# Pairwise feature products on one core: engine programs written as loops, and features copied by GpSimd ahead of the transposes

## Chip, cores and metric

The kernel runs on one core of one Trainium2 chip. The metric is the device time of one execution in microseconds; three runs of the kernel before gave 505.67, 505.77 and 505.79 us, a median of 505.77.

## What is computed

The input `r_x` holds 512 samples of 40 features with 128 numbers each, and `L0_rec_W` is a 128x128 matrix, all in fp32. Each feature is multiplied by the matrix, and then each of the 780 pairs of different features is multiplied element by element. The output has 512 x 780 x 128 numbers, 204.47 MB.

```python
proj = jnp.einsum('bnd,ed->bne', x, W)
out = proj[:, PAIR_I, :] * proj[:, PAIR_J, :]   # all i < j of 40
```

## The kernel before

The 512 samples are four **tiles** of 128, one sample to a partition. A tile's 40 features are 20 **groups** of two, and are worked from the last feature to the first. All x stays in one SBUF tensor, `feats`; the projected features are written over x in place.

The stages run on different engines and are tied by counting semaphores.

- **SP** issues the loads first: tile 0 in three pieces (features 36 to 39, 28 to 35, 0 to 27, L99), then tiles 1 to 3 (L101). After that it issues one store for each **chunk** of 65 pairs, 12 to a tile and 48 in all, once VectorE has it ready (L106 to L108). All these transfers are in SP's queue, in this order.
- **TensorE** transposes the two features of a group into PSUM (`turn`, L122, reading `feats`), and multiplies the transposed features of the group before by the turned matrix (`project`, L128). The two steps alternate, with two buffers for each. For tile 0 it waits for the pieces, and for the rest once for all of tiles 1 to 3 (L157).
- **ACT** (ScalarE) copies each transposed group out of PSUM to `x_turned` (L174), and each projected group back into `feats` (L180).
- **VectorE** (DVE) multiplies. A chunk is made of 2 to 11 `tensor_tensor` instructions (L197), each for one feature i and a run of features j, with both inputs in `feats`; 49 to a tile. The chunk goes to one of three output buffers, `products`, and needs the store of three chunks before to have landed (L207, L212). Within a chunk it waits on `proj_ready` where an instruction needs a group not yet seen (L196). Tile 0 is written out; tiles 1 to 3 are a loop on the chip (L209).
- **GpSimd** (POOL) makes the identity matrix for the transposes (L115, L117) and then does nothing.

TensorE's and ACT's programs for all 80 groups are written out, one instruction after another.

## Time and profile before

| | before |
|---|---|
| median of 3 runs | 505.77 us |
| the profiled execution, its own time | 505.62 us |
| its span in the profile | 503.8 us |
| VectorE busy | 433.6 us (86%), 196 instructions |
| TensorE, ACT busy | 63.4 us, 54.2 us |
| GpSimd busy | 0.7 us, 6 instructions |
| moved by DMA | 215.11 MB, mean 427 GB/s |

The span runs from the first to the last event of the profiled execution; 1.8 us of its own time lie outside of it. Busy shares are averages over the whole span: TensorE and ACT do all their work in the first 80 us. The time of TensorE's matmuls is modelled, and the span of a GpSimd instruction is rough.

### The profile page before, as it was taken

What the parts mean: (1) busy time and instruction counts of PE and PEld (TensorE: products, weight loads), DVE (VectorE), ACT (ScalarE), POOL (GpSimd) and SP (SyncE); (2) the same over time, 40 slices, a digit from 0 to 9 for tenths busy, and PEclk for the clock granted to TensorE, in tenths of its full rate; (3) what the DMA queues carried; (4) which work ended last, traced back from release to release, by engine and by line L of the source; (5) the groups of instructions that cost most, each with busy time, mean ns of one, the idle gap of its engine ahead of it and who ended that gap; (6) DMA issues with size and microseconds to landing.
All of it is one profiled execution on the core that took longest, in us unless ns stands there. A gap on an engine that the chain in (4) does not pass through costs nothing.

```text
span 503.8 us, 1684 instructions
## 1 busy us (share of the span) xinstructions
PE 63.4 (13%) x481; PEld 57.6 (11%) x481; DVE 433.6 (86%) x196; ACT 54.2 (11%) x162; POOL 0.7 (0%) x6
## 2 busy tenths in 40 slices
PE   6659993000000000000000000000000000000000
PEld 5648982000000000000000000000000000000000
DVE  3987899899899989998898999899899989998930
ACT  5638982000000000000000000000000000000000
POOL 0000000000000000000000000000000000000000
PEclk9969997555555555555555555555555555555555
DMA  8999999999999999999999999999999999999997
GB/s 356 424 403 441 427 424 429 447 428 425 434 444 428 428 433 444 428 428 431 447 428 428 431 447 428 428 431 441 433 428 428 436 439 431 428 428 439 433 433 312
DMA packets 7926, 215.11 MB, mean 427 GB/s; under 512 B 880, under 2 KB 1008, under 8 KB 1264
## 3 DMA queue, kind: packets, MB, share of 16 engines
q1 hardware_dynamic: 7776, 214.96, 99.3%
q8 instruction: 4, 0.07, 0.0%
q10 hardware_dynamic: 144, 0.07, 0.0%
q14 instruction: 2, 0.02, 0.0%
HBM read 10.55 MB, written 204.47 MB: 427 GB/s over the span
## 4 chain that ended last, share of the span: by engine, by line
DMA 62%; DVE 25%; issue 5%; DVEq 2%; PE 1%; ACT 0%
DMA out_dram<-products 62%; DVE products L197 25%; DVEq L57 2%; DMA w_in<-in_L_rec_W_dram 1%; PE proj_ps L134 0%; PE turned_ps L125 0%; DVEq L197 0%; DVEq L196 0%; DVEq L209 0%; PE w_ps L143 0%; ACT feats L180 0%; DVEq L212 0%
## 5 line engine op out<-in xcount | busy, mean ns | idle before, releaser
L197 DVE TENSOR_TENSOR products<-feats 128x1280 f32 (+36 forms) x196 | 433.6, 2275 | 49.2 <-DMA out_dram<-products 41.1
L134 PE MATMUL proj_ps<-w_turned,x_turned 128*128 128x128 f32 x320 | 54.7, 295 | 0.6 <-ACT x_turned L174 0.5
L134 PEld LDWEIGHTS proj_ps<-w_turned,x_turned 128*128 128x128 f32 x320 | 43.3, 197 | 5.3 <-ACT x_turned L174 2.1
L125 PE MATMUL turned_ps<-identity,feats 128*128 128x128 f32 x160 | 31.7, 285 | 11.3 <-DMA feats<-in_r_x_dram 10.3
L174 ACT COPY x_turned<-turned_ps 128x256 f32<-128x256 f32 x80 | 30.0, 377 | 12.3 <-PE turned_ps L125 12.1
L180 ACT COPY feats<-proj_ps 128x256 f32<-128x256 f32 x80 | 29.8, 373 | 10.0 <-PE proj_ps L134 4.7
L125 PEld LDWEIGHTS turned_ps<-identity,feats 128*128 128x128 f32 x160 | 20.9, 148 | 12.3 <-issue 10.5
L170 ACT ACT_TABLE_LOAD x1 | 1.3, 1283 | 1.2 <-PEq L224 1.2
L143 PE MATMUL w_ps<-identity,w_in 128*128 128x128 f32 x1 | 0.4, 447 | 4.2 <-DMA w_in<-in_L_rec_W_dram 4.2
L143 PEld LDWEIGHTS w_ps<-identity,w_in 128*128 128x128 f32 x1 | 0.2, 182 | 4.2 <-issue 4.2
L170 ACT COPY w_turned<-w_ps 128x128 f32<-128x128 f32 x1 | 0.3, 266 | 2.3 <-PE w_ps L143 2.3
L117 POOL TENSOR_SCALAR_AFFINE_SELECT identity<-identity 128x128 f32<-128x128 f32 x1 | 0.3, 294 | 0.2 <-POOL identity L115 0.2
L115 POOL MEMSET identity<- 128x128 f32 x1 | 0.2, 204 | 0.3 <-POOLq L224 0.3
L224 POOL MEMSET const-bfloat16-1.0<- 128x1 bf16 x1 | 0.1, 102 | 0.0
L224 POOL MEMSET const-uint8-127<- 128x1 uint8 x1 | 0.1, 102 | 0.0
L224 POOL MEMSET const-float32-1.0<- 128x1 f32 x1 | 0.1, 99 | 0.0
L224 POOL MEMSET const-float32-0.0<- 128x1 f32 x1 | 0.1, 98 | 0.2 <-issue 0.2
## 6 DMA issues: line engine op xcount, KB each, us to landing
out_dram<-products SPq DMA_DIRECT2D x48, 4160.0 KB, 20.5
feats<-in_r_x_dram SPq DMA_DIRECT2D x3, 2560.0 KB, 19.5
feats<-in_r_x_dram SPq DMA_DIRECT2D x1, 1792.0 KB, 8.3
feats<-in_r_x_dram SPq DMA_DIRECT2D x1, 512.0 KB, 4.3
feats<-in_r_x_dram SPq DMA_DIRECT2D x1, 256.0 KB, 3.2
w_in<-in_L_rec_W_dram ACTq DMA_DIRECT2D x1, 64.0 KB, 3.3
```

What stands on the lines that cost most here:

```text
L57: with ExitStack() as ctx:
L115: pool.memset(identity[:, :], 0.0).then_inc(identity_zeroed, 1)
L117: pool.affine_select(out=identity[:, :], in_=identity[:, :], compare_op=ALU.not_equal, fill=1.0, base=0, pattern=[[-1, P]], channel_multip ...
L125: last = pe.transpose(turned_ps[group % 2][:, n - a, :], feats[:, tile, n, :], identity[:, :])
L134: last = pe.matmul(proj_ps[group % 2][:, k, :], x_turned[group % 2][:, k, :], w_turned[:, :], start=True, stop=True)
L143: pe.transpose(w_ps[:, :], w_in[:, :], identity[:, :]).then_inc(w_in_ps, 1)
L170: act.copy(w_turned[:, :], w_ps[:, :]).then_inc(w_ready, 1)
L174: act.copy(x_turned[group % 2][:, :, :], turned_ps[group % 2][:, 0:GROUP, :]).then_inc(x_turned_ready, 1)
L180: act.copy(feats[:, tile, a:b, :], proj_ps[group % 2][:, 0:GROUP, :]).then_inc(proj_ready, 1)
L197: last = dve.tensor_tensor(products[k % SLOTS][:, place:place + count, :], feats[:, tile, i:i + 1, :].broadcast_to([P, count, DIM]), feats ...
L224: nc = _bacc.Bacc("TRN2", target_bir_lowering=False, num_devices=1)
```

## The change

TensorE's and ACT's 80 groups become loops on the chip of two groups a turn, with what does not fit the loop ahead of it and behind it. An instruction of such a loop names the same place on every turn, so GpSimd first copies each group's two features from `feats` to one of two fixed buffers, `staged`, and TensorE's transposes read that. GpSimd waits for the transposes of two groups before (`group_turned`, which starts at 2), and for the loads: the pieces of the first tile worked on, and then once for the three other tiles. VectorE's four tiles are one loop; it waits for projected groups once at a chunk's start, for all that the chunk needs, where it waited between the instructions of a chunk. The first waits that had no count behind them are met by counts given in advance (`proj_ready` starts at 2), and TensorE's wait for `proj_ready` is there for every group. The tiles are worked from the last to the first, so `feats` is walked in falling order. The loads of the first tile now count on the semaphores of the three output buffers.

```diff
-        feats = sbuf("feats", [P, tiles, FEATURES, DIM])
+        feats = sbuf("feats", [P, features, DIM])
         products = [sbuf(f"products{s}", [P, CHUNK, DIM]) for s in range(SLOTS)]
+
+        staged = [sbuf(f"staged{k}", [P, GROUP, DIM]) for k in range(2)]
...
-            for k, (a, b) in enumerate(FIRST_LOADS):
-                sp.dma_start(feats[:, 0, a:b, :], x[0:P, a:b, :]).then_inc(first_loaded[k], 16)
-            for tile in range(1, tiles):
-                sp.dma_start(feats[:, tile, :, :], x[tile * P:(tile + 1) * P, :, :]).then_inc(tiles_loaded, 16)
-
-            for tile in range(tiles):
+            last = (tiles - 1) * P
+            for s, (a, b) in enumerate(PIECES):
+                at = (tiles - 1) * FEATURES
+                sp.dma_start(feats[:, at + a:at + b, :], x[last:last + P, a:b, :]).then_inc(slot_free[s], 16)
+            for tile in reversed(range(tiles - 1)):
+                sp.dma_start(feats[:, tile * FEATURES:(tile + 1) * FEATURES, :],
+                             x[tile * P:(tile + 1) * P, :, :]).then_inc(tiles_loaded, 16)
+
+            for turn in range(tiles):
+                tile = tiles - 1 - turn
                 for k in range(CHUNKS):
                     low, high = chunk_range(k)
-                    sp.wait_ge(chunk_ready, tile * CHUNKS + k + 1)
+                    sp.wait_ge(chunk_ready, turn * CHUNKS + k + 1)
                     sp.dma_start(out[tile * P:(tile + 1) * P, low:high, :],
-                                 products[k % SLOTS][:, :, :]).then_inc(stored[k % SLOTS], 16)
+                                 products[k % SLOTS][:, :, :]).then_inc(slot_free[k % SLOTS], 16)
 
             for slot in range(SLOTS):
-                sp.wait_ge(stored[slot], 16 * tiles * ROUNDS)
+                sp.wait_ge(slot_free[slot], 16 + 16 * tiles * ROUNDS)
...
+            def stage_two(pair):
+
+                for k in range(2):
+                    pool.wait_ge(group_turned, pair * 2 + (k + 1))
+                    pool.tensor_copy(staged[k][:, :, :],
+                                     feats[:, bass.ds(pair * -(2 * GROUP) + (features - (k + 1) * GROUP), GROUP), :]
+                                     ).then_inc(group_staged, 1)
+
+            pairs = [(FEATURES - a) // (2 * GROUP) for a, b in PIECES]
+            pool.wait_ge(slot_free[0], 16)
+            with pool.Fori(0, pairs[0]) as pair:
+                stage_two(pair)
...
+            pool.wait_ge(tiles_loaded, 16 * (tiles - 1))
+            with pool.Fori(pairs[2], groups // 2) as pair:
+                stage_two(pair)
...
-            def turn(tile, group):
-                a, b = group_range(group)
-                for n in range(a, b):
-                    last = pe.transpose(turned_ps[group % 2][:, n - a, :], feats[:, tile, n, :], identity[:, :])
+            def turn(group, k):
+
+                pe.wait_ge(group_staged, group + 1)
+                for n in range(GROUP):
+                    last = pe.transpose(turned_ps[k][:, n, :], staged[k][:, n, :], identity[:, :])
                 last.then_inc(group_turned, 1)
 
-            def project(before, group):
-                pe.wait_ge(x_turned_ready, before + (group + 1))
-                if group >= 2:
-
-                    pe.wait_ge(proj_ready, before + (group - 1))
-                for k in range(GROUP):
-                    last = pe.matmul(proj_ps[group % 2][:, k, :], x_turned[group % 2][:, k, :], w_turned[:, :],
+            def project(group, k):
+                pe.wait_ge(x_turned_ready, group + 1)
+                pe.wait_ge(proj_ready, group + 1)
+                for n in range(GROUP):
+                    last = pe.matmul(proj_ps[k][:, n, :], x_turned[k][:, n, :], w_turned[:, :],
                                      start=True, stop=True)
                 last.then_inc(group_projected, 1)
 
-            def last_banks_left(before):
-                pe.wait_ge(proj_ready, before + GROUPS)
-
+            pe.sem_inc(group_turned, 2)
             pe.wait_ge(identity_made, 1)
             pe.wait_ge(w_loaded, 16)
             pe.transpose(w_ps[:, :], w_in[:, :], identity[:, :]).then_inc(w_in_ps, 1)
-
-            starts = {group_of(b - 1): k for k, (a, b) in enumerate(FIRST_LOADS)}
-            pe.wait_ge(first_loaded[0], 16)
             turn(0, 0)
             pe.wait_ge(w_ready, 1)
-            for group in range(1, GROUPS):
-                if group in starts:
-                    pe.wait_ge(first_loaded[starts[group]], 16)
-                turn(0, group)
-                project(0, group - 1)
-            project(0, GROUPS - 1)
-            last_banks_left(0)
-
-            pe.wait_ge(tiles_loaded, 16 * (tiles - 1))
-            for tile in range(1, tiles):
-                turn(tile, 0)
-                for group in range(1, GROUPS):
-                    turn(tile, group)
-                    project(tile * GROUPS, group - 1)
-                project(tile * GROUPS, GROUPS - 1)
-                last_banks_left(tile * GROUPS)
+            with pe.Fori(0, groups // 2 - 1) as pair:
+                turn(pair * 2 + 1, 1)
+                project(pair * 2, 0)
+                turn(pair * 2 + 2, 0)
+                project(pair * 2 + 1, 1)
+            turn(groups - 1, 1)
+            project(groups - 2, 0)
+            project(groups - 1, 1)
...
+            act.sem_inc(proj_ready, 2)
...
-            def carry_turned(tile, group):
-                act.wait_ge(group_turned, tile * GROUPS + group + 1)
-                act.copy(x_turned[group % 2][:, :, :], turned_ps[group % 2][:, 0:GROUP, :]).then_inc(x_turned_ready, 1)
-
-            def carry_projected(tile, group):
-
-                a, b = group_range(group)
-                act.wait_ge(group_projected, tile * GROUPS + group + 1)
-                act.copy(feats[:, tile, a:b, :], proj_ps[group % 2][:, 0:GROUP, :]).then_inc(proj_ready, 1)
-
-            for tile in range(tiles):
-                carry_turned(tile, 0)
-                for group in range(1, GROUPS):
-                    carry_turned(tile, group)
-                    carry_projected(tile, group - 1)
-                carry_projected(tile, GROUPS - 1)
+            def carry_turned(group, k):
+                act.wait_ge(group_turned, group + 3)
+                act.copy(x_turned[k][:, :, :], turned_ps[k][:, 0:GROUP, :]).then_inc(x_turned_ready, 1)
+
+            def carry_projected(group, k):
+
+                act.wait_ge(group_projected, group + 1)
+                act.copy(feats[:, bass.ds(group * -GROUP + (features - GROUP), GROUP), :],
+                         proj_ps[k][:, 0:GROUP, :]).then_inc(proj_ready, 1)
+
+            carry_turned(0, 0)
+            with act.Fori(0, groups // 2 - 1) as pair:
+                carry_turned(pair * 2 + 1, 1)
+                carry_projected(pair * 2, 0)
+                carry_turned(pair * 2 + 2, 0)
+                carry_projected(pair * 2 + 1, 1)
+            carry_turned(groups - 1, 1)
+            carry_projected(groups - 2, 0)
+            carry_projected(groups - 1, 1)
...
-            def multiply_chunk(tile, k, seen):
-
-                for i, j, count, place in chunk_rows(*chunk_range(k)):
-                    if group_of(i) >= seen:
-                        seen = group_of(i) + 1
-                        dve.wait_ge(proj_ready, tile * GROUPS + seen)
-                    last = dve.tensor_tensor(
-                        products[k % SLOTS][:, place:place + count, :],
-                        feats[:, tile, i:i + 1, :].broadcast_to([P, count, DIM]),
-                        feats[:, tile, j:j + count, :], ALU.mult)
-                last.then_inc(chunk_ready, 1)
-                return seen
-
-            seen = 0
-            for k in range(CHUNKS):
-                if k >= SLOTS:
-                    dve.wait_ge(stored[k % SLOTS], 16 * (k // SLOTS))
-                seen = multiply_chunk(0, k, seen)
-            with dve.Fori(1, tiles) as tile:
-                seen = 0
+            with dve.Fori(0, tiles) as turn:
+                at = turn * -FEATURES + (tiles - 1) * FEATURES
                 for k in range(CHUNKS):
-                    dve.wait_ge(stored[k % SLOTS], 16 * ROUNDS * tile + 16 * (k // SLOTS))
-                    seen = multiply_chunk(tile, k, seen)
+                    dve.wait_ge(slot_free[k % SLOTS], turn * (16 * ROUNDS) + 16 * (k // SLOTS + 1))
+                    if k == 0 or groups_for(k) > groups_for(k - 1):
+                        dve.wait_ge(proj_ready, turn * GROUPS + (2 + groups_for(k)))
+                    for i, j, count, place in chunk_rows(k):
+                        last = dve.tensor_tensor(
+                            products[k % SLOTS][:, place:place + count, :],
+                            feats[:, bass.ds(at + i, 1), :].broadcast_to([P, count, DIM]),
+                            feats[:, bass.ds(at + j, count), :], ALU.mult)
+                    last.then_inc(chunk_ready, 1)
```

VectorE's instructions, their sizes and their order within a tile, the sizes of the loads and the 48 stores are the same.

On TensorE, the start of its program before; the names are the PSUM buffers written and the operands read:

```order
L143 MATMUL w_ps<-identity,w_in 128x128 [waits w_loaded,identity_made]
L125 MATMUL turned_ps0<-identity,feats 128x128 [waits first_loaded0]
L125 MATMUL turned_ps0<-identity,feats 128x128
L125 MATMUL turned_ps1<-identity,feats 128x128 [waits w_ready]
L125 MATMUL turned_ps1<-identity,feats 128x128
L134 MATMUL proj_ps0<-w_turned,x_turned0 128x128 [waits x_turned_ready]
L134 MATMUL proj_ps0<-w_turned,x_turned0 128x128
L125 MATMUL turned_ps0<-identity,feats 128x128 [waits first_loaded1]
L125 MATMUL turned_ps0<-identity,feats 128x128
```

The loop of the change on TensorE, whole:

```order
L159 MATMUL turned_ps1<-identity,staged1 128x128 [waits group_staged]
L159 MATMUL turned_ps1<-identity,staged1 128x128
L163 REGISTER_ALU
L166 MATMUL proj_ps0<-w_turned,x_turned0 128x128 [waits proj_ready,x_turned_ready]
L166 MATMUL proj_ps0<-w_turned,x_turned0 128x128
L157 REGISTER_ALU
L159 MATMUL turned_ps0<-identity,staged0 128x128 [waits group_staged]
L159 MATMUL turned_ps0<-identity,staged0 128x128
L166 MATMUL proj_ps1<-w_turned,x_turned1 128x128 [waits proj_ready,x_turned_ready]
L166 MATMUL proj_ps1<-w_turned,x_turned1 128x128
L176 REGISTER_ALU
L176 COMPARE_AND_BRANCH
```

The transposes read `staged` and wait for it; their order against the projections is as before.

On GpSimd, which had nothing after the identity matrix, the loop of the change for the groups of the three later tiles (30 turns; the loops for the first tile's pieces are alike):

```order
L150 UNCONDITIONAL_BRANCH [waits tiles_loaded]
L150 ISA
L135 ISA [waits group_turned]
L135 COPY staged0<-feats 128x256
L134 REGISTER_ALU
L135 ISA [waits group_turned]
L135 COPY staged1<-feats 128x256
L150 REGISTER_ALU
L150 COMPARE_AND_BRANCH
```

The wait for the loads has moved here from TensorE, and each group adds one copy of 128 x 256 numbers.

On VectorE, the first chunk of the first tile before:

```order
L197 TENSOR_TENSOR products0<-feats 128x128 [waits proj_ready]
L197 TENSOR_TENSOR products0<-feats 128x256 [waits proj_ready]
L197 TENSOR_TENSOR products0<-feats 128x384
L197 TENSOR_TENSOR products0<-feats 128x512 [waits proj_ready]
L197 TENSOR_TENSOR products0<-feats 128x640
L197 TENSOR_TENSOR products0<-feats 128x768 [waits proj_ready]
```

And in the change:

```order
L214 ISA
L219 ISA [waits slot_free0]
L221 ISA [waits proj_ready]
L221 ISA
L221 TENSOR_TENSOR products0<-feats 128x128
L221 ISA
L221 TENSOR_TENSOR products0<-feats 128x256
L221 ISA
L221 TENSOR_TENSOR products0<-feats 128x384
```

One wait for six groups stands ahead of the chunk in place of six waits within it, and an address is set before each multiply.

## Rows read from the trace of the kernel before

**Rows 1.** The page: span, and its slices of DMA share and rate.

```profile
span 503.8 us, 1684 instructions
...
DMA  8999999999999999999999999999999999999997
GB/s 356 424 403 441 427 424 429 447 428 425 434 444 428 428 433 444 428 428 431 447 428 428 431 447 428 428 431 441 433 428 428 436 439 431 428 428 439 433 433 312
```

**Rows 2.** DMA queues: packets, MB, share of 16 engines.

```profile
q1 hardware_dynamic: 7776, 214.96, 99.3%
q8 instruction: 4, 0.07, 0.0%
...
q14 instruction: 2, 0.02, 0.0%
```

**Rows 3.** Stretches: length, busy time (instructions) by engine, TensorE clock, DMA share, GB/s.

```profile
0.00:2.00 2.00, 0.00 (x0) 0.00 (x0) 0.00 (x0) 0.84 (x1) 0.70 (x6) 1.00 0.13 17
2.00:4.00 2.00, 0.00 (x0) 0.00 (x0) 0.00 (x0) 0.44 (x1) 0.00 (x0) 1.00 0.91 288
25.00:26.00 1.00, 0.00 (x0) 0.00 (x0) 1.00 (x2) 0.00 (x0) 0.00 (x0) 0.50 1.34 369
26.00:27.00 1.00, 0.00 (x0) 0.00 (x0) 1.00 (x2) 0.00 (x0) 0.00 (x0) 0.50 0.92 246
27.00:28.00 1.00, 0.00 (x0) 0.00 (x0) 1.00 (x2) 0.00 (x0) 0.00 (x0) 0.50 0.91 335
28.00:29.00 1.00, 0.00 (x0) 0.00 (x0) 1.00 (x1) 0.00 (x0) 0.00 (x0) 0.50 0.75 320
40.00:480.00 440.00, 38.02 (x304) 34.50 (x302) 403.12 (x174) 33.27 (x102) 0.00 (x0) 0.55 1.00 433
```

**Rows 4.** Timeline of VectorE: start, length, what, count, idle before and its releaser.

```profile
7.21 0.29 DVE L197 TENSOR_TENSOR products<-feats 128x128 f32<-128x128 f32 x1 [7.21 <-ACT feats L180]
8.28 27.40 DVE L197 TENSOR_TENSOR products<-feats 128x256 f32<-128x256 f32 x21 [0.77 <-ACT feats L180]
41.04 9.03 DVE L197 TENSOR_TENSOR products<-feats 128x1920 f32<-128x1920 f32 x4 [5.36 <-DMA out_dram<-products]
50.86 8.96 DVE L197 TENSOR_TENSOR products<-feats 128x2048 f32<-128x2048 f32 x3 [0.79 <-DMA out_dram<-products]
...
90.20 8.96 DVE L197 TENSOR_TENSOR products<-feats 128x1024 f32<-128x1024 f32 x3 [0.86 <-DMA out_dram<-products]
```

**Rows 5.** Waits: who waited for whom, us in total, times, longest.

```profile
DVE products L197 <- DMA out_dram<-products: 41.1, 42, 5.4
```

**Rows 6.** The page's issues: KB each, median us from issue to landing.

```profile
out_dram<-products SPq DMA_DIRECT2D x48, 4160.0 KB, 20.5
```

**Rows 7.** The page's groups of VectorE and GpSimd: busy, mean ns of one, idle before.

```profile
L197 DVE TENSOR_TENSOR products<-feats 128x1280 f32 (+36 forms) x196 | 433.6, 2275 | 49.2 <-DMA out_dram<-products 41.1
...
L117 POOL TENSOR_SCALAR_AFFINE_SELECT identity<-identity 128x128 f32<-128x128 f32 x1 | 0.3, 294 | 0.2 <-POOL identity L115 0.2
L115 POOL MEMSET identity<- 128x128 f32 x1 | 0.2, 204 | 0.3 <-POOLq L224 0.3
L224 POOL MEMSET const-bfloat16-1.0<- 128x1 bf16 x1 | 0.1, 102 | 0.0
```

**Rows 8.** Timeline of ACT, TensorE and SP, same columns as rows 4.

```profile
10.87 0.37 ACT L180 COPY feats<-proj_ps 128x256 f32<-128x256 f32 x1
...
11.60 0.37 ACT L180 COPY feats<-proj_ps 128x256 f32<-128x256 f32 x1
...
12.32 0.37 ACT L180 COPY feats<-proj_ps 128x256 f32<-128x256 f32 x1
...
17.61 18.42 SPq L107 DMA_DIRECT2D out_dram<-products  x3
...
31.31 1.09 PE L125 MATMUL turned_ps<-identity,feats 128*128 128x128 f32 x4 [10.34 <-DMA feats<-in_r_x_dram]
```

More of the change, by code:

```diff
@@ L14 @@
 GROUPS = FEATURES // GROUP
-FIRST_LOADS = [(36, 40), (28, 36), (0, 28)]
+PIECES = [(36, 40), (28, 36), (0, 28)]
 SLOTS = 3
@@ L23, with chunk_rows @@
 ROUNDS = CHUNKS // SLOTS
-assert CHUNKS * CHUNK == PAIRS and ROUNDS * SLOTS == CHUNKS
-assert GROUPS * GROUP == FEATURES and GROUPS % 2 == 0 and GROUP <= BANK_FEATURES
-def group_range(group):
-    return FEATURES - (group + 1) * GROUP, FEATURES - group * GROUP
-def group_of(i):
-    return (FEATURES - 1 - i) // GROUP
+assert CHUNKS * CHUNK == PAIRS and ROUNDS * SLOTS == CHUNKS and len(PIECES) == SLOTS
+assert GROUPS * GROUP == FEATURES and GROUPS % 2 == 0 and 2 * GROUP <= BANK_FEATURES
 def chunk_range(k):
     return PAIRS - (k + 1) * CHUNK, PAIRS - k * CHUNK
-def chunk_rows(low, high):
+def chunk_rows(k):
+    low, high = chunk_range(k)
     rows = []
@@ L48, in chunk_rows, with groups_for @@
     return rows
+def groups_for(k):
+    return (FEATURES - 1 - chunk_rows(k)[-1][0]) // GROUP + 1
 def pairwise_products(nc, x, w, out):
@@ L55, in pairwise_products @@
     assert x.shape[0] == tiles * P and 2 <= tiles <= 4
+    features = tiles * FEATURES
+    groups = tiles * GROUPS
     with ExitStack() as ctx:
@@ L79, in pairwise_products @@
         w_loaded = sem("w_loaded")
-        first_loaded = [sem(f"first_loaded{k}") for k in range(len(FIRST_LOADS))]
+        slot_free = [sem(f"slot_free{s}") for s in range(SLOTS)]
         tiles_loaded = sem("tiles_loaded")
@@ L86, in pairwise_products @@
         w_ready = sem("w_ready")
+        group_staged = sem("group_staged")
         group_turned = sem("group_turned")
@@ L91, in pairwise_products @@
         chunk_ready = sem("chunk_ready")
-        stored = [sem(f"stored{s}") for s in range(SLOTS)]
         block = ctx.enter_context(nc.Block())
@@ new lines, in _ @@
+            pool.wait_ge(slot_free[0], 16)
+            with pool.Fori(0, pairs[0]) as pair:
+                stage_two(pair)
+            pool.wait_ge(slot_free[1], 16)
+            with pool.Fori(pairs[0], pairs[1]) as pair:
+                stage_two(pair)
+            pool.wait_ge(slot_free[2], 16)
+            with pool.Fori(pairs[1], pairs[2]) as pair:
+                stage_two(pair)
+            pool.wait_ge(tiles_loaded, 16 * (tiles - 1))
+            with pool.Fori(pairs[2], groups // 2) as pair:
+                stage_two(pair)
```

## The prediction

> **What bounds the kernel now.** I read the page's slices first. The 16 DMA engines are at 0.9 or more of the time in every slice but the first and the last [rows 1], and SP's queue, which holds all loads and stores, takes 99.3% of what they can give [rows 2]. From 40 to 480 us they move 433 GB/s at a share of 1.00 [rows 3]. So the kernel runs at the pace of its stores, and the question is whether the queue ever runs dry.
>
> VectorE's timeline gives the rhythm. Its chunks begin at 41.04, 50.86, 60.69 and, three chunks on, 90.20 us, each time when a store has landed [rows 4]: one store each (90.20 - 41.04) / 5 = 9.83 us. Store number n (from 0) lands at 41.04 + 9.83n, so the 48th at 503.1, which is the span. VectorE takes 8.96 to 9.03 us for such a chunk and then idles 0.79 to 0.87 us; 41.1 us of its idle time are waits for stores [rows 4, 5]. A store takes 20.5 us from issue to landing [rows 6], two stores' time, so when VectorE ends a chunk the DMA engines still have the rest of one store and a whole one before them. That is the cover: VectorE may fall behind by some 10 us before the engines stop, and it wins back about 0.8 us with each chunk.
>
> TensorE and ACT are far ahead of need: a group each 0.73 us (copies at 10.87 and 11.60), and TensorE idles 10.34 us until tiles 1 to 3 are there at 31.31 [rows 8].
>
> **The parts that cost nothing by themselves.** *Tiles in falling order, loads on other semaphores*: the same loads in the same order of sizes, the same stores in SP's queue, nothing ahead of them: 0. *TensorE and ACT as loops*: register steps and a branch, some tenths of a us for two groups. If a group took 1.5 us in place of 0.73, 80 would take 120 us and VectorE needs them over 400 us; it is hidden, and it stays hidden as long as VectorE finds its groups. *VectorE's addresses*: tiles 1 to 3 had them already, and ran at the pace of the stores. *The waits at a chunk's start*: VectorE began at 7.21 us, after the first group; now it must have six. ACT's copy of the sixth began at 10.87 and took 0.37 us [rows 8], which is 11.24, and with GpSimd's copy ahead of the transposes and a few register steps I put VectorE's start at 11.7. Three chunks before took from 8.28 to 35.68, with a pause of 5.36 us behind them until the first store had landed at 41.04 [rows 4]. From 11.7 they end near 39, inside that pause. The first store was issued at 17.61 [rows 8]; now it would be near 21, while the loads run until 31.3. So this costs nothing alone, but it spends most of that pause. *The wait for the loads*, now GpSimd's, stops the same groups as it did in TensorE.
>
> **The part that can cost: 80 copies on GpSimd.** No row has GpSimd and VectorE at work together, so the price is bounded. Of one copy, 128x256: a MEMSET of one column takes 102 ns and one of 128 columns 204, that is 0.80 ns a column more, and AFFINE_SELECT, which also reads, 294 ns for 128 columns, 1.5 ns a column [rows 7]. So 256 columns take 0.31 to 0.49 us. TensorE waits for the copy, but a group every 0.8 to 1 us is still enough. What matters is VectorE: both engines read `feats` in SBUF. If they don't hinder each other, the copies cost nothing. If they take turns, a multiply waits for the copy that got in between. Then VectorE loses at least the 0.31 us less the 0.10 us that even one column takes, 0.21; at most 0.49 us and the overlap of two multiplies behind each other as well. That overlap: 196 x 2.275 = 445.9 us of instructions are 433.6 us of busy time [rows 7], 12.3 us over the 148 joints inside chunks, 0.08 us each. The ends are 0.21 and 0.57 us; nearest to a copy that reads and writes lies no row, so I take the middle, 0.39.
>
> **The sum, if they take turns (my forecast).** VectorE is busy without a pause once it is behind, and one copy gets in at each of its multiplies. The first 20 groups are done by 31.3 us (only the first six before VectorE starts); the other 60 then go one to a multiply. Chunks 0 and 1 have 17 multiplies, and 17 + 60 = 77 is reached in chunk 16 (49 in the first tile, 29 in the five chunks 12 to 16). So 74 copies stand in VectorE's way before the end of chunk 16. It ends at 11.7 + 17 x 9.05 + 74s = 165.6 + 74s, with 9.05 us a chunk from the busy time, 433.6 / 48 = 9.03, and a little between. To keep the engines fed it must be issued before store 15 lands, at 41.04 + 9.83 x 15 = 188.5, less the 1.5 us that a transfer takes to begin (the first load was issued at 0.74; the engines have a share of 0.13 up to 2 us and 0.91 from 2 to 4 [rows 3]): 187.0. The loss is 74s - 21.4: at s = 0.39 it is 7.5 us, at 0.57 20.8 us, and nothing below s = 0.29. After chunk 16 VectorE wins back 0.8 us a chunk, but time that the DMA engines stood idle does not come back.
>
> The profiled execution took 505.62 us, 0.15 below the median of 505.77. 505.6 + 7.5 = **513.1 us**. This case's own range is 505.6 to 526.4.
>
> [...]
>
> **The rivals.**
>
> *Side by side.* The two engines don't hinder each other. For it: all of TensorE's, ACT's and VectorE's work from 40 to 60 us ran beside each other and a chunk took 8.96 us, as it did from 90 us on when they were done [rows 4]. Against it: that says nothing of GpSimd. Time 505.6 to 505.8.
>
> *VectorE keeps its place.* A copy gets in only when VectorE pauses. There is one pause a chunk, 0.8 us, room for a copy; a tile needs 20 groups and has 12 chunks. So VectorE comes to a chunk whose groups are missing and waits for them at 0.75 to 1 us each. For a tile this needs 15 to 20 us of pauses where 12 x 0.83 = 10 are free: 5 to 10 us lost for each of three tiles, less the cover of 10 us that is there once and less the groups of the first tile that were done early: 0 to 15 us, 505.6 to 520, middle 510.
>
> *Faster: the engines get back what they miss between 25 and 29 us.* In these four microseconds they moved 369, 246, 335 and 320 GB/s where 433 is their pace [rows 3]: 0.46 MB, 1.1 us. If fetching the long programs is what stands in the way (6 packets of instructions, 0.09 MB [rows 2]), short loops take it away: 504.5. It decides as soon as one such packet sits on the engine that ends last. Against it: the packets are 0.09 of 215 MB, 0.2 us at 433 GB/s, and loads and stores change over in just this stretch. [...]
>
> **How the numbers follow.** A measurement of this kernel can tell 0.2%, 1.0 us. Chances: taking turns 0.52, of which a fifth falls below s = 0.30 and can't be told from no change; side by side 0.28; VectorE keeps its place 0.13, two thirds of it slower; faster 0.07. Slower: 0.42 + 0.09 = 0.51. Same: 0.10 + 0.28 + 0.04 = 0.42. Faster: 0.07. The predicted time is that of the likeliest case, 513.1. The range takes in the first rival and the first case's upper bound with a little for the delays between the engines that no row prices: 505.2 to 528.
>
> **What the profile would show.** Taking turns: copies on GpSimd whose spans run from 0.3 up to a multiply's length, VectorE's start-to-start times longer by about 0.4 us while the copies last, TensorE's and ACT's last group near 190 us instead of 80, no pauses of VectorE between 31 and 190 us, DMA shares under 0.9 in some slices there, and from 190 us on the rhythm of before. Side by side: the last group before 100 us, multiplies at their old pace and a pause again before each chunk. VectorE keeping its place: pauses that end with ACT's copy to `feats`, spread to the end of the run. Faster: no dip between 25 and 29 us. The forecast is wrong if a copy takes far from 0.4 us, if VectorE starts well after 12 us (the first store then comes after the loads have ended and each us late is a us lost), or if two copies get in at one multiply.

## The result, and the profile after

| | before | after |
|---|---|---|
| median of 13 runs each, on one chip | 505.71 us | 506.81 us |
| ratio, with its 95% interval | | 1.0025 (1.0018 to 1.0032) |
| the profiled execution, its own time | 505.62 us | 506.74 us |
| its span | 503.8 us | 504.9 us |
| instructions executed | 1684 | 2550 |
| GpSimd busy | 0.7 us | 159.3 us |

The change costs about 1.1 us. The direction is the forecast one; the size was forecast at 7.5 us. The profile shows nearly all that the forecast case describes, and yet not its loss. This is the page of the kernel after: the span, busy times, the slices of VectorE, GpSimd, ACT and DMA share, queues, the two costliest groups of the engines in question, and the stores.

```profile
span 504.9 us, 2550 instructions
PE 100.6 (20%) x481; PEld 84.7 (17%) x481; DVE 446.2 (88%) x196; ACT 59.8 (12%) x162; POOL 159.3 (32%) x86
...
DVE  0999999999999999998899999899999989998930
ACT  4623222222443200000000000000000000000000
POOL 3969999999799900000000000000000000000000
...
DMA  8999999999999999999999999999999999999996
...
q1 hardware_dynamic: 7776, 214.96, 99.1%
...
q14 instruction: 1, 0.01, 0.0%
...
L221 DVE TENSOR_TENSOR products<-feats 128x1280 f32 (+30 forms) x196 | 446.2, 2343 | 37.7 <-DMA out_dram<-products 24.4
L135 POOL COPY staged<-feats 128x256 f32 (+1 forms) x80 | 158.6, 2024 | 16.5 <-DMA feats<-in_r_x_dram 10.4
...
out_dram<-products SPq DMA_DIRECT2D x48, 4160.0 KB, 20.3
```

GpSimd is busy in 14 slices of 12.6 us, up to 177 us, and ACT as long: before, ACT was done at 80. VectorE's multiplies are busy for 12.6 us more in all [rows 7]. But the DMA share is 0.9 or more in all slices but the first and the last, as before [rows 1]: VectorE's delay never let the queue run dry. The time is lost while the DMA engines look full.

Three views show the form of the delay. First GpSimd's copy alone, in a window before VectorE starts, and then beside VectorE (count: min/median/max in ns, where in us, shapes):

```profile
L135 POOL COPY staged<-feats x6: 397/403/404, 4.1 to 8.8; 128x256 f32 x4, 128x256 f32<-128x256 f32 x2
...
L135 POOL COPY staged<-feats x5: 1921/3656/3922, 59.8 to 72.9; 128x256 f32 x5
```

A copy that takes 0.40 us alone spans a whole multiply beside VectorE: it gets in once for each. VectorE's timeline, and ACT's last group (start, length, what, count, idle before):

```profile
13.17 175.61 DVE L221 TENSOR_TENSOR products<-feats 128x128 f32 x81 [13.17 <-ACT feats L199]
...
189.43 8.96 DVE L221 TENSOR_TENSOR products<-feats 128x2048 f32 x3 [0.64 <-DMA out_dram<-products]
199.26 8.96 DVE L221 TENSOR_TENSOR products<-feats 128x1280 f32 x3 [0.87 <-DMA out_dram<-products]
...
179.06 0.37 ACT L199 COPY feats<-proj_ps 128x256 f32<-128x256 f32 x1 [0.48 <-PE proj_ps L166]
```

VectorE works without a pause from 13.17 to 188.8 us, 81 multiplies of chunks 0 to 17, and the pauses before chunks return at 189.43. Third, stretches that hold one chunk of 3 large multiplies (stretch, length, VectorE's busy time and instructions, TensorE's granted clock, DMA share, GB/s; the x5 counts the neighbours that touch the stretch too): beside the copies, and after them.

```profile
63.10:72.57 9.47, 9.47 (x5) 0.50 0.99 425
...
189.43:198.39 8.96, 8.96 (x3) 0.50 1.03 446
```

The 189.43 chunk is undisturbed: 8.96 us. A chunk beside the copies takes 9.55 us from its first multiply to its last's end, and 9.47 from start to start. So a copy costs VectorE (9.55 - 8.96) / 3 = **0.197 us** a multiply. That is half of what the prediction took for it.

Single stores, first stores 9 and 15 of the kernel before, then stores 0, 9 and 15 of the kernel after and the issue of its store 16 (issue in ns, and where; then time to landing):

```profile
L107 SPq DMA_DIRECT2D out_dram<-products x1: 333/333/333, 109.0 to 109.0; - x1
DMA to landing us min/median/max: 20.5/20.5/20.5
...
L107 SPq DMA_DIRECT2D out_dram<-products x1: 332/332/332, 168.1 to 168.1; - x1
DMA to landing us min/median/max: 20.4/20.4/20.4
```

```profile
L118 SPq DMA_DIRECT2D out_dram<-products x1: 348/348/348, 24.3 to 24.3; - x1
DMA to landing us min/median/max: 15.5/15.5/15.5
...
L118 SPq DMA_DIRECT2D out_dram<-products x1: 332/332/332, 110.6 to 110.6; - x1
DMA to landing us min/median/max: 17.8/17.8/17.8
...
L118 SPq DMA_DIRECT2D out_dram<-products x1: 333/333/333, 170.5 to 170.5; - x1
DMA to landing us min/median/max: 18.8/18.8/18.8
...
L118 SPq DMA_DIRECT2D out_dram<-products x1: 332/332/332, 179.9 to 179.9; - x1
```

Here is where the time goes. Store 0 lands at 39.8 us (before: 41.0) and store 9 at 128.4 (129.5): the kernel after is 1.1 us *ahead*. Store 15 lands at 189.3 (188.5): it is 0.8 behind. And the last lands at 504.5 (503.4). From landing to landing the kernel before takes 9.83 us all along; the one after takes 9.83 up to store 8, then 9.93, 10.41, 10.24, 10.19, 10.13 and 10.10 for stores 9 to 14, and then 9.88 and 9.84 again. Chunk 16 is ready and its store issued at 179.9, 7.1 us ahead of the 187.0 that the forecast asked of it. Each of the first 17 stores was issued at least 5.6 us before the one ahead of it had landed. Nothing was late at the queue, and yet the queue took longer.

### The profile page after: what moved, and what is told of

It is laid out like the page before. It is cut to its first block, busy times and chain, and to the rows that moved or that the text cites. A ratio compares the mean times of both kernels' runs of the same rounds, so it can differ in the third digit from the quotient of the medians.

```text
span 504.9 us, 2550 instructions
## 1 busy us (share of the span) xinstructions
PE 100.6 (20%) x481; PEld 84.7 (17%) x481; DVE 446.2 (88%) x196; ACT 59.8 (12%) x162; POOL 159.3 (32%) x86
## 4 chain that ended last, share of the span: by engine, by line
DMA 41%; DVE 39%; issue 11%; DVEq 3%; PE 2%; ACT 0%; ACTq 0%
DMA out_dram<-products 40%; DVE products L221 39%; DVEq L58 2%; DVEq L221 1%; PE proj_ps L166 1%; DMA w_in<-in_L_rec_W_dram 1%; PE turned_ps L159 1%; DVEq L214 0%; PE w_ps L173 0%; DVEq L217 0%; ACT feats L199 0%; DVEq L219 0%; ACTq L199 0%
## 5 line engine op out<-in xcount | busy, mean ns | idle before, releaser
L221 DVE TENSOR_TENSOR products<-feats 128x1280 f32 (+30 forms) x196 | 446.2, 2343 | 37.7 <-DMA out_dram<-products 24.4
L135 POOL COPY staged<-feats 128x256 f32 (+1 forms) x80 | 158.6, 2024 | 16.5 <-DMA feats<-in_r_x_dram 10.4
L166 PE MATMUL proj_ps<-w_turned,x_turned 128*128 128x128 f32 x320 | 72.7, 372 | 0.0
L166 PEld LDWEIGHTS proj_ps<-w_turned,x_turned 128*128 128x128 f32 x320 | 65.2, 283 | 1.2 <-ACT x_turned L194 0.9
L159 PE MATMUL turned_ps<-identity,staged 128*128 128x128 f32 x160 | 46.8, 388 | 74.1 <-POOL staged L135 73.7
L159 PEld LDWEIGHTS turned_ps<-identity,staged 128*128 128x128 f32 x160 | 22.9, 185 | 88.6 <-POOL staged L135 88.4
L199 ACT COPY feats<-proj_ps 128x256 f32 (+1 forms) x80 | 29.8, 373 | 34.2 <-PE proj_ps L166 33.8
```

The lines of the kernel that those rows point to most:

```text
L135: pool.tensor_copy(staged[k][:, :, :], feats[:, bass.ds(pair * -(2 * GROUP) + (features - (k + 1) * GROUP), GROUP), :]).then_inc(group_sta ...
L159: last = pe.transpose(turned_ps[k][:, n, :], staged[k][:, n, :], identity[:, :])
L166: last = pe.matmul(proj_ps[k][:, n, :], x_turned[k][:, n, :], w_turned[:, :], start=True, stop=True)
L199: act.copy(feats[:, bass.ds(group * -GROUP + (features - GROUP), GROUP), :], proj_ps[k][:, 0:GROUP, :]).then_inc(proj_ready, 1)
L221: last = dve.tensor_tensor(products[k % SLOTS][:, place:place + count, :], feats[:, bass.ds(at + i, 1), :].broadcast_to([P, count, DIM]), ...
```

## The experiments

All kernels compute the full output; those named "beside" only add work. Each is compared with runs of the kernel before on the same chip, whose medians lay at 505.70 to 505.75. Differences in us are to these. Every trace shown is that of one execution, while a kernel's time is the median of its 2 to 13 runs.

### GpSimd's copies moved to ACT

`act_stages` is the kernel after, with the copies to `staged` in ACT's loop and nothing on GpSimd.

```diff
-                    pool.tensor_copy(staged[k][:, :, :], feats[...]).then_inc(group_staged, 1)
+            def stage(group, k):
+                act.copy(staged[k][:, :, :], feats[...]).then_inc(group_staged, 1)
...
+                with act.Fori(first, end) as pair:
+                    stage(pair * 2 + 2, 0)
                     carry_turned(pair * 2 + 1, 1)
```

> The changed kernel with the 80 copies to staged made by ACT instead of GpSimd; loops and everything else as in the change. Theory A (each GpSimd copy stops VectorE for 0.20 us, which the queue's cover hides; the 1.1 us that the change is slower is a late DMA engine, slowed while GpSimd's loop runs to 177 us, against 1.2 us won because TensorE's program is no longer fetched during the loads): VectorE's chunks of three multiplies take 8.96 us again and pause 0.8 us before each; the last group is done before 130 us; the first store still lands near 39.8 us; time 504.3 to 505.5, faster than the kernel before. Rival B (the loops themselves, or VectorE's later start, cost it): 506.5 to 507.5 as the change.

It took 507.19 us, +1.5, ratio 1.0031 (1.0019 to 1.0044). VectorE's timeline:

```profile
70.61 8.96 DVE L212 TENSOR_TENSOR products<-feats 128x2048 f32 x3 [1.39 <-DMA out_dram<-products]
81.10 8.96 DVE L212 TENSOR_TENSOR products<-feats 128x1280 f32 x3 [1.52 <-DMA out_dram<-products]
91.59 8.96 DVE L212 TENSOR_TENSOR products<-feats 128x1024 f32 x3 [1.53 <-DMA out_dram<-products]
...
111.37 8.96 DVE L212 TENSOR_TENSOR products<-feats 128x2048 f32 x3 [0.88 <-DMA out_dram<-products]
```

My theory's 504.3 to 505.5 us is missed. The time is the one that the rival's text gives. VectorE isn't disturbed (8.96) and pauses 1.39 to 1.53 us before each chunk, and still the kernel is 0.4 us slower than the one with the copies on GpSimd. From 70.61 to 91.59 a store takes 10.49 us, at 111.37 the pause is back to 0.88. ACT's last group ends near 93 us. So it isn't VectorE's delay that costs the time: stores are slow, 10.49 us each, while the loops run.

### The copies alone, put into the kernel before

`before_staged` keeps all programs written out and adds GpSimd's 80 copies, which TensorE reads.

```diff
+                pool.tensor_copy(staged[g % 2][:, :, :], feats[:, tile, a:b, :]).then_inc(group_staged, 1)
...
-                    last = pe.transpose(turned_ps[group % 2][:, n - a, :], feats[:, tile, n, :], identity[:, :])
+                    last = pe.transpose(turned_ps[group % 2][:, n - a, :], staged[group % 2][:, n - a, :],
```

> The kernel before, its TensorE and ACT programs written out, with only the GpSimd copies to staged added (written out too). Theory A: VectorE loses 0.20 us per copy as in the change, no pauses from 41 to about 180 us; TensorE's program is fetched again (q8 packets), so the first store lands near 41 us; time 505.7 to 508, at or above the change. Rival B (loops cost, not copies): 505.7, as before, within 0.2.

506.15 us, +0.45, ratio 1.0007 (0.9998 to 1.0016): no difference that can be told, and at most 0.8 us. The copies by themselves aren't the whole loss. VectorE's chunks take 9.36 us here, with a pause of 0.45 to 0.51 us before them in which one copy runs alone: one copy to a multiply, and one to a pause.

### Copies of twice the size

`wide_copies` is the kernel after with each copy writing its group twice, 512 columns in place of 256.

```diff
-                    pool.tensor_copy(staged[k][:, :, :], feats[...])
+                    group = feats[...]
+                    pool.tensor_copy(staged[k][:, :, :, :], group.unsqueeze(1).broadcast_to([P, 2, GROUP, DIM]))
```

> The changed kernel with each GpSimd copy twice as wide (the group is written twice, 512 columns). Theory A: the stall of VectorE per copy grows with the columns read, from 0.20 to about 0.40 us; by the sum of the prediction the loss is 74 x 0.40 - 21.4 = 8.2 us, so 513 to 516. Rival C (the stall is a fixed handover, whatever the copy's length): 0.20 us again and 506.5 to 507.5.

515.30 us, +9.6, ratio 1.0189 (1.017 to 1.0207). Its page, its group of copies, and the stretch of one chunk:

```profile
span 513.5 us, 2550 instructions
...
L136 POOL COPY staged<-feats 128x512 f32 (+1 forms) x80 | 174.9, 2230 | 9.6 <-DMA feats<-in_r_x_dram 5.8
```

```profile
68.76:78.87 10.11, 10.11 (x5) 0.50 0.98 421
```

From start to start a chunk takes 10.11 us, where it was 9.47 with 256 columns. 256 more columns cost (10.11 - 9.47) / 3 = 0.21 us a multiply, so s = 0.41. The sum of the prediction then gives 74 x 0.41 - 21.4 = 8.9 us; measured were 9.6, in two runs. Chunk 16's store was issued at 194.8 us, 7.8 after the 187.0 of the prediction. Here the DMA engines do stand idle (length; busy time and instructions of TensorE, its weight loads, VectorE, ACT, GpSimd; clock, DMA share, GB/s):

```profile
45.00:50.00 5.00, 3.53 (x17) 3.23 (x16) 5.00 (x3) 1.81 (x5) 5.00 (x3) 0.50 0.74 320
150.00:160.00 10.00, 5.58 (x31) 4.57 (x30) 10.00 (x7) 4.06 (x12) 9.93 (x7) 0.83 0.75 319
```

They ran dry for the first time when chunk 2's store came at 48.2 us, not only at chunk 16. So the sum's total comes close, and its price for 256 columns was wrong; that it comes so close is in part luck, for VectorE's start 1.3 us later than it assumes, and the price of instructions found below, are in the 9.6 us and not in the sum.

### The change without its copies, TensorE written out

`pe_unrolled`: TensorE's program has no loop and reads `feats`, GpSimd does nothing; ACT and VectorE stay loops. Those two loops move their place in `feats` from turn to turn. TensorE's loop reads fixed buffers in every kernel here that has it, so that it needs the copies isn't shown.

```diff
-                pe.wait_ge(group_staged, group + 1)
-                    last = pe.transpose(turned_ps[k][:, n, :], staged[k][:, n, :], identity[:, :])
+                    at = features - (group + 1) * GROUP + n
+                    last = pe.transpose(turned_ps[k][:, n, :], feats[:, at, :], identity[:, :])
```

> The change without GpSimd's copies and with TensorE's program written out, reading feats; ACT's loop, VectorE's single loop, its waits at a chunk's start and the falling order of tiles stay. Theory A: these parts cost nothing, 505.5 to 506.0, first store lands near 41 us. Rival B: the loops of ACT and VectorE and its later start are what cost: over 506.4.

506.49 us, +0.8, ratio 1.0017 (1.0008 to 1.0026). With no copy and no GpSimd work, most of the loss, 0.8 of 1.1 us, is still there; the time is just above 506.4, the rival's lower bound. The three kernels that aren't held up by VectorE's pace stand in the order of one number of the page, the instructions executed, where register steps, branches and waits count too: 1770 gave +0.45, 2034 +0.8, 2390 +1.5. The kernel after, with 2550, falls out of the row at +1.1.

I then went to the records of single DMA packets. The trace of `before` has 864 packets of 4 bytes, 16 for each of the 54 loads and stores of SP's queue, and a step of the store's semaphore a median of 0.35 us behind each one's end. I take each for the end of one DMA engine's part; store 0 landed at 41.02 us, 0.36 behind its 16th. The offsets of the two latest engines, in us behind the first engine's end of store 0, less 9.835 us a store (worked out from the trace's 4-byte packets):

| store | 0 | 3 | 6 | 9 | 12 | 14 | 47 |
|---|---|---|---|---|---|---|---|
| before: latest, second | 3.03, 1.19 | 3.02, 2.50 | 3.01, 2.49 | 3.00, 2.48 | 2.99, 2.47 | 2.99, 2.48 | 3.03, 2.92 |
| after: latest, second | 2.38, 0.48 | 2.37, 0.96 | 2.35, 1.65 | 2.34, 2.27 | 3.63, 2.34 | 4.17, 2.34 | 4.70, 2.22 |

The records don't name the engine; one is known again by its offset, which changes little or steadily from store to store.

A store has 128 packets of 33280 bytes, with a median of 1.232 us each in `before`; 8 of them take 9.86 us, about a store's 9.83, so I take it that each of the 16 engines moves 8. In the kernel before a fixed one is last up to about store 34 (3.03 at store 0, 2.92 at 34). But another one falls behind while the compute engines work, and hardly any more when only VectorE's few large multiplies are left. In the kernel before it goes from 0.67 at store 1 to 2.27 at store 4, creeps on, and is the latest at the end (3.03 against 2.92). In the kernel after it overtakes at store 9 or 10, where the landings begin to slow, and its steep drift ends near 177 us, with GpSimd's loop. At the last store it is 4.70 behind, the latest engine of before 3.03, which is 1.67 more; the first engine had ended store 0 earlier by 0.59 (39.78 - 2.38 against 41.02 - 3.03). 1.67 - 0.59 = 1.08 us: this is the measured loss. In `pe_unrolled` this engine ends at 3.66, in `act_stages` at 5.06. So the new theory: **each executed instruction, a register step or a branch too, holds this one DMA engine up a little.** From the first runs that is some 2.3 ns.

Single stores of the kernel after bear it out. Between the landings of stores 9 to 14 start 228, 165, 140, 112 and 107 instructions, and these five landings take 0.58, 0.41, 0.36, 0.30 and 0.27 us more than 9.83: 2.5 to 2.7 ns an instruction. From store 1 to store 47 the engine falls back by 2.36 us in the kernel before, with 974 instructions, and by 4.22 in the kernel after, with 1735: 2.4 ns in both.

### Instructions that do nothing

`steps_beside` is the kernel before with 4000 instructions on GpSimd that touch no data: 1000 turns with waits that are met (four in the source, two executed instructions), a register step and a branch. `bare_steps` has 2000 turns with a step and a branch alone.

```diff
+            pool.wait_ge(tiles_loaded, 16 * (tiles - 1))
+            with pool.Fori(0, 1000):
+                for _ in range(4):
+                    pool.wait_ge(identity_made, 1)
```

```diff
+            with pool.Fori(0, 2000):
+                pass
```

> The kernel before, with a loop of 1000 turns added on GpSimd after the loads, of register steps, branches and satisfied waits only: no copy, no data. Theory D (one of the 16 DMA engines is held up by about 2.3 ns for each instruction that the engines execute, and the stores wait for the slowest DMA engine: read from the 60 later groups, 900 instructions and 2.1 us in the kernel before, 1140 and 2.7 with TensorE written out, 1420 and 3.1 with ACT's copies): the loop is 2000 to 6000 instructions, so 3.5 to 13 us slower than the kernel before, 509 to 519, with VectorE's chunks at 8.96 us and its pauses before them longer than 0.8 us while the loop runs. Rival E (data moved by the copies, or TensorE's and ACT's reads and writes, are what holds the DMA engine up): 505.7, within 0.3.

> The kernel before, with an empty loop of 2000 turns on GpSimd after the loads: a register step and a branch to a turn, 4000 instructions, and no semaphore in it. Theory D (every executed instruction holds the same DMA engine up by 2.3 ns, of whatever kind): 9.3 us slower if the loop lies wholly inside the run, 514 to 516. Rival F (it is the semaphore waits, 2000 of the 4000 instructions of the earlier loop): 505.7 to 506.5.

515.08 us, +9.3, ratio 1.0187 (1.0171 to 1.0202), and 515.89 us, +10.2, 1.0209 (1.0193 to 1.0224). The page of the first and its VectorE timeline:

```profile
span 513.3 us, 5685 instructions
```

```profile
192.19 8.96 DVE L201 TENSOR_TENSOR products<-feats 128x2048 f32 x3 [0.93 <-DMA out_dram<-products]
202.28 8.96 DVE L201 TENSOR_TENSOR products<-feats 128x1280 f32 x3 [1.13 <-DMA out_dram<-products]
212.40 8.96 DVE L201 TENSOR_TENSOR products<-feats 128x1024 f32 x3 [1.17 <-DMA out_dram<-products]
...
242.65 8.89 DVE L201 TENSOR_TENSOR products<-feats 128x3328 f32 x2 [1.12 <-DMA out_dram<-products]
```

VectorE's multiplies are undisturbed and its pauses longer: (242.65 - 192.19) / 5 = 10.09 us a store. This shows the cause by itself: an engine that moves no data makes the stores 2.6% slower. 9.33 us / 4001 instructions = 2.33 ns each. In the packets the one engine ends 12.7 us behind. That waits aren't needed for it the second kernel shows. Its four runs took 515.15, 515.16, 516.63 and 516.90: two lie where the first kernel's do, and the median is the middle between the pairs. Why two are 1.5 longer with the same instructions is not known.

### Copies and memsets that share nothing with VectorE

Both are the kernel before with 100 chained instructions of 128x256 on GpSimd, on tensors of their own: copies in a loop, or memsets written out.

```diff
+            with pool.Fori(0, 50) as turn:
+                for k in range(2):
+                    pool.wait_ge(junk_done, turn * 2 + (k + 1))
+                    pool.tensor_copy(junk_to[:, 0:GROUP * DIM], junk_from[...]).then_inc(junk_done, 1)
```

```diff
+            for turn in range(100):
+                if turn:
+                    pool.wait_ge(junk_done, turn)
+                pool.memset(junk_to[:, :], 0.0).then_inc(junk_done, 1)
```

> The kernel before, with 100 copies of 128x256 numbers from a tensor of their own to another added on GpSimd after the loads, each waiting for the one before. Taking turns: one copy to each multiply, VectorE loses 0.20 us each, so chunks of three multiplies take 9.55 us from 31 us on, and the copies last until about chunk 20; a copy's span is as long as the multiply beside it. The cover holds (100 x 0.2 = 20 us against 0.8 us regained a chunk and 10 at the start): 505.7 to 507.5. If only the sharing of `feats` mattered, no stall: chunks of 8.96 us and the copies over by 75 us.

> The same with 100 memsets of 128x256 in place of the copies: GpSimd writes and reads nothing. Theory (it is the read that VectorE's second input and GpSimd share): memsets take 0.31 us each, are over by about 75 us, and VectorE's chunks stay at 8.96 us; 505.7 to 506.3. Rival (any use of SBUF by GpSimd stops VectorE): 9.55 us as with copies.

506.73 us, +1.0, and 506.11 us, +0.4. Their groups, the stretch of a chunk beside the copies, and VectorE's timeline beside the memsets:

```profile
L128 POOL COPY junk_to<-junk_from 128x256 f32 x100 | 208.5, 2085 | 45.2 <-DMA feats<-in_r_x_dram 29.6 <-POOL junk_to L128 15.6
```

```profile
199.41:208.88 9.47, 9.47 (x5) 0.50 1.03 446
```

```profile
L125 POOL MEMSET junk_to<- 128x256 f32 x100 | 31.1, 311 | 35.2 <-DMA feats<-in_r_x_dram 29.5
```

```profile
50.62 8.96 DVE L204 TENSOR_TENSOR products<-feats 128x2048 f32<-128x2048 f32 x3 [0.80 <-DMA out_dram<-products]
60.45 8.96 DVE L204 TENSOR_TENSOR products<-feats 128x3328 f32<-128x3328 f32 x3 [0.86 <-DMA out_dram<-products]
```

Copies of a private tensor take VectorE the same 9.47 us a chunk, and last as long as a multiply. Memsets keep their 0.31 us and take VectorE nothing. So GpSimd's copies take turns with VectorE, out of `feats` or out of a private tensor (9.47 us both), and its memsets, which only write, don't (8.96). I read from this that it is GpSimd's reading. Every multiply here has both inputs in SBUF, so what the second input has to do with it isn't shown. The times are near those of 403 and 100 more instructions at 2.3 ns, 0.9 and 0.2; the second can't be told from no change (ratio 1.0008, 0.9999 to 1.0018).

### Fewer instructions

If the count costs time, less of it must give some back. `groups_of_four` is the kernel before with four features to a group, 1534 instructions in place of 1684.

```diff
-GROUP = 2
+GROUP = 4
```

> The kernel before with groups of four features instead of two: as many matmuls, half as many copies of ACT (each twice as wide), half as many waits. Theory D: some 100 to 150 fewer instructions; the store that ends last may come 0.2 to 0.3 us earlier, and not more, since the late DMA engine of the kernel before got its 3 us during the loads: 505.2 to 505.8. Rival B: no relation to the count of instructions, 505.7.

505.36 us, -0.39, ratio 0.9992 (0.9983 to 1.0001); the rule says -0.35. The sign and size fit, but the interval touches 1.

### A later first store

The kernel after had its store 0 landed 1.2 us earlier than before although it was issued at 24.3 in place of 17.6. I took the later issue for the reason. `chunk_waits` is the kernel before with VectorE's waits at a chunk's start, `four_chunk_waits` the same with `GROUP = 4`.

```diff
+                needed = group_of(chunk_rows(*chunk_range(k))[-1][0]) + 1
+                if needed > seen:
+                    seen = needed
+                    dve.wait_ge(proj_ready, tile * GROUPS + seen)
...
-                    if group_of(i) >= seen:
```

> The kernel before with one part of the change: VectorE waits for all the groups that a chunk needs at the chunk's start. Theory G (the first store, issued at 17.6 us among the loads, makes the slowest DMA engine later at the loads' end; issued after 21 us it doesn't): the first store is issued near 21 us and lands at 39.5 to 40.5 us instead of 41.0, but the engine that the instructions hold up then decides, so the whole gains at most 0.3 us: 505.3 to 505.8. Rival B (a later start of VectorE costs): 506 to 508.

> The same with groups of four features, some 150 instructions fewer than the kernel before. By theories D and G together the last store lands earlier by 0.2 to 0.6 us than in the kernel before: 505.0 to 505.5, faster than both kernels. If either is wrong: 505.4 (as groups of four alone) or more.

505.73 us, 0.0, ratio 1.0001 (0.9992 to 1.001); and 505.36 us, -0.4, ratio 0.9994 (0.9985 to 1.0003), no more than `groups_of_four` alone. The first has its store 0 issued at 21.2 and landed at 40.5, 0.6 before the kernel before, and gained nothing. The theory isn't borne out: `steps_beside` issues its store 0 at 18.2 and has it landed at 39.1, so the issue doesn't set the landing.

The trace of `chunk_waits` shows more. It is that of its slowest execution, 507.58 us, 1.9 above the median:

```profile
span 505.8 us, 1664 instructions
...
50.77 8.96 DVE L198 TENSOR_TENSOR products<-feats 128x2048 f32<-128x2048 f32 x3 [1.27 <-DMA out_dram<-products]
61.19 8.96 DVE L198 TENSOR_TENSOR products<-feats 128x3328 f32<-128x3328 f32 x3 [1.46 <-DMA out_dram<-products]
71.52 8.96 DVE L198 TENSOR_TENSOR products<-feats 128x2048 f32<-128x2048 f32 x3 [1.36 <-DMA out_dram<-products]
81.81 8.96 DVE L198 TENSOR_TENSOR products<-feats 128x1280 f32<-128x1280 f32 x3 [1.33 <-DMA out_dram<-products]
```

With no more instructions than the kernel before, its landings are up to 10.4 us apart here. The drifting engine is already 2.84 us behind at store 1, where it is 0.67 in the kernel before and at most 0.5 in the kernel after, and ends at 5.06. From store 1 to 47 it drifts by 2.22 us with 948 instructions, again 2.3 ns. So the drift goes by the instructions, and where it starts from can differ by 2 us; what sets that isn't known, nor whether one kernel's executions differ by as much. No kernel of this study is faster than the kernel before by more than its interval.

### All together

| kernel | instructions | difference, us | 2.33 ns x instructions more |
|---|---|---|---|
| four_chunk_waits | 1529 | -0.4 | -0.4 |
| groups_of_four | 1534 | -0.4 | -0.3 |
| chunk_waits | 1664 | 0.0 | 0.0 |
| before_staged | 1770 | +0.5 | +0.2 |
| memsets_beside | 1784 | +0.4 | +0.2 |
| pe_unrolled | 2034 | +0.8 | +0.8 |
| copies_beside | 2087 | +1.0 | +0.9 |
| act_stages | 2390 | +1.5 | +1.6 |
| **after** | 2550 | +1.1 | +2.0 |
| steps_beside | 5685 | +9.3 | +9.3 (taken from it) |
| bare_steps | 5685 | +10.2 | +9.3 |

The price is taken from one kernel and fits eight of the other ten within 0.3 us. Differences under some 0.5 us lie within their intervals. The kernel after is 0.9 below; it is this kernel that came to store 9 1.1 us ahead. From store 1 on it follows the price: its engine drifts 1.86 us more than in the kernel before, with 761 instructions more. The rest, -0.78, was there by store 1.

## Why the prediction was right and wrong

- **The direction.** Slower, as forecast, and inside the stated range, but this is luck: the wait that the forecast priced cost nothing, and what made the kernel 1.1 us slower was not in the prediction.
- **What bounds the kernel.** Right: the stores set the pace, and each microsecond lost is lost there. No slice under 0.9 came, which the forecast case had asked for.
- **Who waits for whom.** Right in form: turn-taking of GpSimd and VectorE, one copy to a multiply, copies as long as a multiply (1.9 to 3.9 us), groups until 179 us in place of 80, no pause of VectorE, and then the old rhythm. A chunk's start-to-start time while the copies last was to be 0.4 us a multiply longer; it is 0.20. No row of before has GpSimd beside VectorE; the chance of 0.52 for this case was an estimate.
- **The price s, the step that failed.** "I take the middle, 0.39." Measured: 0.197, just under the low bound of 0.21. That bound was built as a memset's 0.31 us less the 0.10 that a single column takes, the time for the columns. Twice the columns cost twice as much (0.41), so the fixed part of GpSimd's instruction is not in it, and neither is the overlap of two multiplies that the upper end added. With 0.197 the term is 74 x 0.197 - 21.4 = -6.8, below zero: nothing lost, as the prediction says of anything under 0.29. The forecast of 7.5 us comes from this number alone, and `wide_copies` shows that at 0.41 such a loss is real.
- **The start.** VectorE started at 13.17 in place of 11.7, the first store was issued at 24.3 and not at 21. That came out of the cover, as forecast, and cost nothing. Worked out with these values, chunk 16 ends at 165.6 + 1.5 + 14.6 = 181.7; it ended at 179.9, which left 7.1 us.
- **"TensorE and ACT as loops: hidden."** Their time is hidden: VectorE never waits for a group between 13.17 and 188.8 us. But the prediction priced instructions by their time on their own engine alone. This is the second step that failed, a term put at nothing: it left out what 866 more executed ones do to a DMA engine, by the price 2.0 us, less the 0.9 that the kernel after was ahead: that is the measured +1.1. The landings of before hide it: they are even, because the engine that drifts there is the latest only from about store 34 on, and then by 0.1 us.
- **The rivals.** Side by side: 505.6 to 505.8, near in time, wrong in form. VectorE keeps its place: no pause that ends with ACT's copy. Faster by the instruction fetches: q8's four packets [rows 2] are gone from the page, where q14 alone is left with one, and no time was gained. Store 0 did land 1.2 us earlier, but it landed earlier still, at 39.5, in `pe_unrolled`, which has q8's four packets again.

## What to carry to other kernels

Price a GpSimd read beside VectorE's multiplies of two SBUF inputs, the only kind here, at its columns alone (0.8 ns each here, from 0.20 us for 256 columns and 0.41 for 512, one instruction to a multiply), and then compare the sum with the cover that the bound resource has: here the 74 copies lost nothing at 0.20 us each, and at 0.41 the loss was 9.6 us where the sum gives 8.9. In a kernel that is bound by DMA over its whole length, count executed instructions too, with each turn's steps, branches and waits: here 1000 of them on GpSimd cost 2.3 us, and those of the other engines' loops fit the same price (`pe_unrolled` +0.8, `act_stages` +1.5), so a loop in place of written-out code can lose time although every engine has time to spare. This is shown for recorded runs alone; whether it holds without the profiler is open. When the busy shares don't explain a difference, compare from landing to landing and look at where the pace changes.

## What was not expected of the hardware

- In these runs one of 16 DMA engines falls behind by about 2.3 ns for each executed instruction, register steps and branches too, and a store ends with the slowest engine (4.70 us behind at the last store of the kernel after). For GpSimd's instructions `steps_beside` (+9.3 us for 4001) and `bare_steps` (+10.2) show it; that those of the other engines cost the same is a fit to the counts. After the loop of `steps_beside`, which ends at 412 us, the landings are 9.84 us apart again. All runs here were recorded by the profiler, so whether it is the instructions themselves or the recording of them isn't known. A run without the profiler would tell.
- VectorE and GpSimd alternate while both have work: one read instruction of GpSimd to one multiply, however long the multiply is (a copy spans 1.9 to 3.9 us between 59.8 and 72.9 us of the kernel after, 0.40 alone). VectorE pays 0.20 us for 256 columns, 0.41 for 512.
- Open: why the landing of store 0 varies from 38.5 to 41.0 us among these kernels, and where the drifting engine stands by then, from under 0.5 to 2.4 us behind; and so why the kernel after lost 0.9 us less than the rule says.
